# Grouping TensorE's products two slots at a time in a four-batch attention and quantised feed-forward layer

## What is computed

```python
x = x + attn(layernorm(x), Wq, Wk, Wv, Wo, bo)     # 16 heads of 64, softmax over 1024 keys, scale 1/8
x = x + ffn(layernorm(x), w_gate, w_up, w_down)    # silu(gate) * up, hidden width 352
```

## Time and profile before

| | |
|---|---|
| median of 3 runs | 1754.97 us (1754.33 to 1756.84) |
| profiled execution | 1758.2 us, of which the span from first to last instruction 1756.4 us |
| busy, share of the span | TensorE 1617.6 us (92%), VectorE 1431.2 (81%), GpSimd 1252.1 (71%), ScalarE 1070.3 (61%) |
| mean granted clock of TensorE | 0.977 of full speed |
| chain of waits that ended last | TensorE 52%, VectorE 41%, ScalarE 3% |
| DMA | 10.6% of the 16 engines' span |

### The profile page before, as it was taken

One profiled execution on the slowest core, in us unless ns is written; L12 is line 12 of the kernel. 1 busy time (PEld: TensorE's weight loads), 2 busy tenths in 40 slices (PEclk: granted clock), 3 DMA queues, 4 the chain that ended last, 5 costly groups with the idle time before them and its releaser, 6 DMA issues.

```text
span 1756.4 us, 35369 instructions
## 1 busy us (share of the span) xinstructions
PE 1617.6 (92%) x13825; PEld 1192.2 (68%) x13825; DVE 1431.2 (81%) x2463; ACT 1070.3 (61%) x2222; POOL 1252.1 (71%) x1369
## 2 busy tenths in 40 slices
PE   4899999999999999999999999999999999999966
PEld 2576677777776667776667776667767676777754
DVE  7777776666788888888888888988888888888777
ACT  3466566666666656666666666665666665666533
POOL 3577777777777777777777777777777777777853
PEclk8899999999999999999999999999999999999987
DMA  5110001111111001111001111000111100111000
GB/s 133 25 25 14 19 20 26 26 25 26 26 26 27 15 15 27 27 26 27 15 16 26 27 27 25 21 20 15 27 27 26 27 15 15 27 27 26 3 4 12
DMA packets 26373, 43.24 MB, mean 25 GB/s; under 512 B 3744, under 2 KB 18016, under 8 KB 26208
## 3 DMA queue, kind: packets, MB, share of 16 engines
q1 hardware_dynamic: 26208, 40.99, 10.6%
HBM read 4.80 MB, written 2.10 MB: 4 GB/s over the span
## 4 chain that ended last, share of the span: by engine, by line
PE 52%; DVE 41%; ACT 3%; issue 2%; POOL 1%; DMA 0%; DVEq 0%; ACTq 0%; POOLq 0%
PE ob L534 14%; DVE negm L767 12%; PE sm L488 10%; PE st L506 7%; PE st L508 7%; PE mb L433 4%; DVE k_l L718 3%; DVE q_hl L718 2%; DVE xn L934 2%; PE mb L449 2%; DVE qv L919 2%; DVE q_small L915 2%; DVE qw L926 2%; PE mb L444 2%; DVE qw L924 2%
## 5 line engine op out<-in xcount | busy, mean ns | idle before, releaser
L381 POOL TENSOR_TENSOR p_low<-probs 128x512 f16<-128x512 f32 x1024 | 1086.0, 1070 | 424.5 <-ACT probs L616 422.6
L616 ACT ACTIVATE probs<-st 128x512 f32<-128x512 f32 x1024 | 607.9, 597 | 423.9 <-PE st L508 421.6
L767 DVE TENSOR_REDUCE negm<-sm 128x1 f32<-128x1024 f32 x512 | 624.6, 1220 | 150.8 <-PE sm L488 147.5
L506 PE MATMUL st<-q_hl,k_hh 128*128 128x512 f32 x1024 | 465.7, 455 | 0.0
L488 PE MATMUL sm<-k_hh,q_hl 128*128 128x512 f32 x1024 | 370.4, 443 | 65.1 <-DVE negm L767 62.4
L508 PE MATMUL st<-q_hm,k_l 66*128 66x512 f32 x1024 | 409.5, 400 | 0.0
L534 PEld LDWEIGHTS ob<-v,probs 128*128 128x128 bf16 x4096 | 236.5, 98 | 141.7 <-issue 141.7
L534 PEld LDWEIGHTS ob<-v,p_low 128*128 128x128 f16 x4096 | 234.8, 97 | 144.0 <-issue 130.2
L534 PE MATMUL ob<-v,probs 128*128 128x129 f16 x4096 | 325.1, 222 | 0.0
L534 PE MATMUL ob<-v,p_low 128*128 128x129 f16 x4096 | 323.0, 221 | 1.8 <-POOL p_low L381 1.8
L506 PEld LDWEIGHTS st<-q_hl,k_hh 128*128 128x128 f32 x1024 | 194.8, 190 | 40.6 <-issue 0.9
(11 more groups left out here) (145 smaller groups left out, 1611.2 us busy)
## 6 DMA issues: line engine op xcount, KB each, us to landing
k_hh<-k_hh SPq DMA_DIRECT2D x64, 256.0 KB, 3.3
q_hm<-q_hl SPq DMA_DIRECT2D x64, 256.0 KB, 3.4
x<-x SPq DMA_DIRECT2D x4, 512.0 KB, 7.2
q_hm<-m_high SPq DMA_DIRECT2D x128, 2.0 KB
q_hm<-m_low SPq DMA_DIRECT2D x128, 2.0 KB
out<-x SPq DMA_DIRECT2D x24, 64.0 KB, 1.5
probs<-wq SPq DMA_DIRECT2D x1, 512.0 KB, 5.6
probs<-wk SPq DMA_DIRECT2D x1, 512.0 KB, 6.8
```

Of the source, the lines that this page charges most:

```text
L381: return pool.tensor_tensor(p_low[b][:, j, :], p, p.bitcast(BF16)[:, 1::2], ALU.subtract)
L506: pe.matmul(st[s % 2][:, :], k_hh[n][:, s * P:(s + 1) * P], q_hl[n][:, half * HALF:(half + 1) * HALF], start=True, stop=False)
L616: nc.scalar.activation(probs[k % 2][:, s, :], st[s % 2][:, :], ACT.Exp, scale=SCALE).then_inc(s_ex, 1)
L767: nc.vector.tensor_reduce(negm[k % 2][:, s // 2:s // 2 + 1], sm[:, :, :].rearrange("p a n -> p (a n)"), AX.X, ALU.max, negate=True).then_i ...
```

## The change

TensorE's part of each unit is reordered. The bodies of ST and V become functions, without any other edit, and a pair of slots is now listed as SM, SM, ST, ST, V, V, jobs. The programs of the other engines, the table JOBS, all the semaphores and the counts waited for are the same.

```diff
-                    for s in range(SLOTS):
-                        slot = 8 * k + s
-                        has_max = cur if k < 2 else nxt
-                        if has_max and s % 2:
-                            scores(s)
-                        if cur:
...
-                        if prev if k == 0 else cur:
...
-                        if has_max and not s % 2:
-                            scores(s)
-                        for n in jobs_at(ON_PE, r, k, s):
-                            job(JOBS[n][0], g, r, q, n)
+                    def scores_t(s):
...
+                        wait(pe, s_ex, 32 * (g - 1) + slot - 1)
...
+                    def values(s):
...
+                    has_max = cur if k < 2 else nxt
+                    for two in range(0, SLOTS, 2):
+                        for s in (two, two + 1):
+                            if has_max:
+                                scores(s)
+                        for s in (two, two + 1):
+                            if cur:
+                                scores_t(s)
+                        for s in (two, two + 1):
+                            if prev if k == 0 else cur:
+                                values(s)
+                        for s in (two, two + 1):
+                            for n in jobs_at(ON_PE, r, k, s):
+                                job(JOBS[n][0], g, r, q, n)
```

More of the change, by code:

```diff
@@ L490, in scores @@
                                   ).then_inc(s_sm, 1)
-                    for s in range(SLOTS):
+                    def scores_t(s):
+                        n = 2 * q + head
                         slot = 8 * k + s
-                        has_max = cur if k < 2 else nxt
-                        if has_max and s % 2:
-                            scores(s)
-                        if cur:
[L499 to L510, removed]
-                        if prev if k == 0 else cur:
[L513 to L538, removed]
-                        if has_max and not s % 2:
-                            scores(s)
-                        for n in jobs_at(ON_PE, r, k, s):
-                            job(JOBS[n][0], g, r, q, n)
@@ new lines, in scores_t @@
+                        if slot == 0:
+                            wait(pe, s_dq, 32 * g)
+                        if s == 0:
+                            wait(pe, s_md[k % 2], 32 * (2 * (g - 1) + k // 2 + 1))
+                        wait(pe, s_ex, 32 * (g - 1) + slot - 1)
+                        pe.matmul(st[s % 2][:, :], k_hh[n][:, s * P:(s + 1) * P],
+                                  q_hl[n][:, half * HALF:(half + 1) * HALF], start=True, stop=False)
+                        pe.matmul(st[s % 2][:, :], k_l1[n][:, s * P:(s + 1) * P],
+                                  q_hm[n][:, half * HALF:(half + 1) * HALF], start=False, stop=True
+                                  ).then_inc(s_st, 1)
@@ new lines, in values @@
+                    def values(s):
+                        pq, ph = (1 - q, 1) if k == 0 else (q, (k - 1) // 2)
+                        bank, low, t = s // 4, s // 2 % 2, 2 * (s // 4) + s % 2
+                        if s % 4 == 0:
+                            wait(pe, s_ob, 2 * (unit - 1) + bank - 1)
+                        if k == 1 and s == 0:
+                            wait(pe, s_v, 2 * g)
+                        for j in range(JT):
+                            if s == 0 and j == 0:
+                                wait(pe, s_ex, 8 * unit - 1)
+                            if s == 0 and j == JT - 1:
+                                wait(pe, s_ex, 8 * unit)
+                            if s == 2 and j == 0:
+                                wait(pe, s_lp, JT * unit)
+                            if low:
+                                p = p_low[1 - k % 2][:, j, t * P:(t + 1) * P]
+                            else:
+                                p = probs[1 - k % 2][:, j, :].bitcast(BF16)[:, 2 * t * P + 1:2 * (t + 1) * P:2]
+                            o = (t % 2) * OT
+                            last = pe.matmul(ob[bank][:, o:o + VC], p, v[pq][:, j, ph, 0:VC],
+                                             start=(j == 0 and s % 4 == 0), stop=(j == JT - 1 and low == 1),
+                                             skip_group_check=True)
+                        if s % 4 == 3:
+                            last.then_inc(s_pv, 1)
```

## The result

The changed kernel takes **1904.95 us**, the median of 4 runs (1902.93 to 1906.46), against 1755.34 (4 runs) of the kernel before. The ratio is 1.0848, with a 95% interval from 1.0834 to 1.0862: 8.5% slower. The forecast was 1845 us in a range of 1800 to 1895. The direction was right, the size was not: 150 us lost instead of 90.

A forecast was written before the change was run, and what follows sets the result against it. TensorE was taken as the bound, tied to VectorE's reduction at SM. Tile rounds +70 us, rounds 5 to 8 +8, 1 to 4 and 9 +13, round 32 -1, total +90: 1845 us, range 1800 to 1895.

The forecast's parts named there:

- The tie: Loop job, VectorE's take, reduction, SM, job: SM to job grows from 1.50 to 2.38 us, 0.88 more each turn.
- the stretches 0 to 4, 4 to 8 and 8 to 12: Slots of round 19 between SMs, lengthened by the later jobs: +0.54, +0.73 and +0.88 us.
- The saved passage: One of two passages from V to a 512-column product goes in each TensorE pair: 0.08 us gained a pair.
- the clock falls too: Rival: the new wait ahead of SM 30 halves TensorE's clock, 1.7 us each; 1882 us once a round, 1920 twice; chance 0.12.
- The total without the clock: Sum over all rounds: +3.16 us in each of 22 tile rounds, the other rounds smaller, +90 us in total.
- 16 to 20: Slots of a tile round: o1's take and the tile's statistics push slot 17's reduction back, +0.60 us on 7.01.
- The low parts get more time: GpSimd's low parts, 1 us each: the V needing them lies later behind its ST, so no loss was counted.
- 20 to 26: Slots of a tile round, bound partly by VectorE's quantisation and partly by TensorE: -0.24 us.
- 26 to 30: Slots of a tile round: job m comes 2.37 us after SM 26, SM 30 4.60 after m; 6.97 against 6.08, +0.89 us.
- The saved passage wins: Rival: no new wait arises in slots 0 to 8, only the passage's gain of 41 us remains, 1714 us; chance 0.08.
- only the chains that already bind: Rival: slots 12, 20 and 30 lose 0.88 us each, the rest gains; +22, 1777 us; chance 0.10.

The follow-up runs named there:

- e_head: Changed kernel with ST and V not grouped, pair order SM SM ST V ST V jobs, SM still at the head: 1911.79 us.
- e_reduce_first: Changed kernel, with VectorE listing each reduction ahead of the even slot's takes instead of behind them: 1894.22 us.
- e_fill: Changed kernel with 4, 5 and 5 extra products ahead of the SM of slots 12, 20 and 30 in rounds 9 to 32: 1847.88 us.
- e_vv: Kernel before with TensorE's pair reordered to V V ST SM SM ST jobs, value products grouped, the two ST apart: 1777.71 us.
- e_tail_single: Kernel before with TensorE's pair reordered to ST V ST V SM SM jobs, SM at the end, ST and V not grouped: 1752.15 us.
- e_tail_pool: e_tail with GpSimd making only 8 of 512 columns of the low parts of slots 25 to 29 from round 9 on: 1715.95 us.
- e_tail: Changed kernel with SM moved to the end of the pair, order ST ST V V SM SM jobs, both groupings kept: 1793.20 us.

## Why the prediction was right and wrong

- **The tie, right.** The prediction had 4.45 us from a job to the next SM but one and 2.38 from SM to the job. For q0 the change has 4.41 and 2.43, and the stretches 0 to 4, 4 to 8 and 8 to 12 came at 7.06, 6.83 and 8.22 against 7.10, 6.83 and 8.15. The plain round was forecast at 48.5 and measured 48.1. A tile round has five waits of SM and not about seven, at the five slots named. e_head shows that the place of SM carries it, e_reduce_first that it is the work ahead of the reduction.
- **The saved passage, right in a row, small in sum.** TensorE in the changed kernel, one pair after a wait:

```profile
1075.22 0.39 PE L502 MATMUL st<-q_hl,k_hh 128*128 128x512 f32 x1
1075.45 0.39 PE L504 MATMUL st<-q_hm,k_l 66*128 66x512 f32 x1
1075.68 0.40 PE L502 MATMUL st<-q_hl,k_hh 128*128 128x512 f32 x1
1075.91 0.40 PE L504 MATMUL st<-q_hm,k_l 66*128 66x512 f32 x1
1076.15 1.08 PE L531 MATMUL ob<-v,probs 128*128 128x129 f16 x16
1077.05 0.71 PE L488 MATMUL sm<-k_hh,q_hl 128*128 128x512 f32 x2
```

  ST products start 0.23 to 0.24 apart, sixteen value products take 0.90 instead of the 0.88 assumed. A dense pair takes 2.37 to 2.40 against 2.45.
- **The step that failed: the clock, a term that the sum put at nothing.** The forecast of 1845 us has no fall of the clock in rounds 10 to 31. The prediction named the case, "the clock falls too", with 37 us for once and 75 for twice a round, gave it 0.12 and closed the range at 1895 with part of it. The runs showed 34 falls in those 22 rounds: at the prediction's price of 1.7 us each 58 us, and e_fill, which takes them away, is 57 us faster. 1845 and 57 are 1902, against 1905 measured. So the price was right and the chance was not. What misled me: I compared only the new wait ahead of slot 30 with the fall in the earlier trace rows and left out slots 12 and 20. By the prediction's own sums these would wait 0.59 + 0.88 = 1.47 and 0.43 + 0.60 = 1.03 us; they waited 1.59 and 1.91, and 22 of the 34 falls came behind them. And nothing had been measured between waits under 1 us, which kept the clock, and the one in the earlier trace rows, where TensorE was busy 1.45 of 3.4 us. Three places in such a gap are more than one chance in eight.
- **The total without the clock, partly luck.** e_fill lost 92 us against 90 in the sum. But a tile round without falls takes 55.66 us, not 55.3, which is 77 us in 22 rounds instead of 70; rounds 5 to 8 lost 7 instead of 8, and rounds 1 to 4 and 9 only 7.5 instead of 13. These misses cancel, and so do those inside the tile round that follow. One reading of the profile was off too, though nothing was worked out from it: TensorE's standing still is not a quarter of the difference between the two kinds of round but nearly half (2.8 less 0.2 us, of 5.6, by the earlier trace rows).
- **16 to 20, mis-sized.** Forecast 7.61, measured 8.44. The late take of o1 did push the reduction of slot 17 back by the expected half (1.31 us after SM instead of 0.76). On top of it xn starts 0.82 us later behind that reduction, by a wait that I had not seen. VectorE and GpSimd in that stretch of the changed kernel:

```profile
1067.52 1.19 DVE L775 TENSOR_REDUCE negm<-sm 128x1 f32<-128x1024 f32 x1
...
1068.09 1.04 POOL L381 TENSOR_TENSOR p_low<-probs 128x512 f16<-128x512 f32 x1 [1.10 <-ACT probs L624]
...
1069.08 0.19 POOL L1013 TENSOR_TENSOR var_eps<-mv,ln_eps 128x1 f32<-128x1 f32 x1
...
1069.94 1.05 DVE L1002 TENSOR_SCALAR xn<-x,mv,rstd 128x128 f32<-128x128 f32 x1 [0.44 <-POOL rstd L1015]
```

  GpSimd's root for the tile (rstd) stands behind the low part of slot 16, which follows an exp that now comes later against SM: the low part starts 1.88 us after SM, before 0.44. "The low parts get more time" was true for V and overlooked what else is in GpSimd's queue.
- **20 to 26 and 26 to 30, mis-sized.** 0.86 less and 0.33 more than forecast. In 20 to 26 a wait went away that I had not counted. Job x of slot 23 stood for the quantised tile in every tile round of the kernel before, as here in round 19; in the change the tile is ready, as TensorE comes later behind its wait of slot 20:

```profile
1003.88 0.30 PE L1014 MATMUL mb<-ident,xn 128*128 128x128 f32 x1 [0.64 <-DVE xn L934]
```

  In 26 to 30, job m comes 2.60 us after SM 26 instead of 2.37, with the long products of g and u right ahead of that SM, and SM 30 comes 4.70 after m instead of 4.60. The 0.10 is the stretch of the quantisation: its two operations on 22 columns and the one on 352 take 1.77 us here together (0.61, 0.18, 0.98) and 1.66 before (0.18, 0.96, 0.52). Together with 16 to 20 the three stretches are only 0.30 us off, which is luck.
- **The rivals.** "The saved passage wins" and "only the chains that already bind" fell with slots 4 and 8, which wait 0.31 and 0.51 us where nothing waited before.

What stays open: why one wait of 1.6 to 1.9 us has a fall behind it and the next, of the same length, has none. Why e_vv is slow was not taken apart. No order of the three kinds of products beat the kernel before by more than e_tail_single's 0.2%; the 2.3% of e_tail_pool leaves out work and only shows what a free GpSimd would be worth.

## What to carry to other kernels

When an order of instructions is changed, follow the rings: from a job through the engine that takes it, back to the instruction at the head of the queue that waits, and on to the next job. Moving a waiting instruction ahead of independent work lengthens each ring by that work, here by 0.88 us. When a forecast makes new waits of TensorE, compare each with the longest ones that kept the full clock and the shortest that lost it; between the two, count the fall in, and try a few idle products in the wait before rebuilding anything.

## What the runs showed of the hardware that was not expected

- More work made the kernel faster: 2 products (0.47 us) in each of three waits a round gave 54 us back, by keeping the granted clock at 1.00.
- Of 66 waits of 1.6 to 1.9 us in otherwise dense work, 34 were followed by a stretch at half the clock, a loss of about 1.6 us each; of 66 waits of 1.1 to 1.4 us none was. Removing one of three such waits a round did not remove falls: 34 stayed 34.
- VectorE's small operations took 0.21 or 0.97 us, and one on 352 columns 0.53 or 1.36 us, by what GpSimd did beside them. Grouping ST and V, which neither engine executes, took the latter from 0.54 to 1.36 us and the pair from slot 28 to 30 from 3.6 to 4.5 us (e_tail_single, e_tail).
